# Projections in straight code with x turned a chunk ahead, and attention's first group loaded in the projection stage

## The reference

```
Q = x @ Wq ; K = x @ Wk ; V = x @ Wv          # Wq, Wk 256x512, Wv 256x256; 16 heads of 2*16 for Q, K
attn = softmax(Q1 K1^T * s) - lamb * softmax(Q2 K2^T * s)
x = layernorm(x + layernorm'(attn V @ Wo))
x = layernorm(x + moe(x))                     # 8 experts, top 2, 256 -> 1024 -> 256
```

## Time and profile before

| | us |
|---|---|
| median of 3 runs | 3537.51 |
| the profiled execution | 3536.64 |
| its span | 3534.9 |
| first projection matmul | 19.83 |
| last PE work of the projection stage starts | 185.64 |
| first instruction of the attention stage | 191.17 |
| first score matmul | 212.56 |
| first transposed scores of the main loop's lead | 266.01 |

### The profile page before, as it was taken

The page is one execution under the profiler, slowest core; times in us unless marked ns, Lnnn a source line. Parts: engine busy times, 40 slices in busy tenths (PEclk is TensorE's granted clock), DMA queues, the critical chain, the costliest instruction groups (busy, mean ns, idle before and its releaser), DMA issues. The chain is left out here.

```text
span 3534.9 us, 85163 instructions
## 1 busy us (share of the span) xinstructions
PE 3161.3 (89%) x29393; PEld 1464.0 (41%) x29394; DVE 2871.0 (81%) x3275; ACT 2510.3 (71%) x4642; POOL 415.4 (12%) x572
## 2 busy tenths in 40 slices
PE   7849999999999999999999999999993645999995
PEld 3413333333333333333333333333332534999994
DVE  2269999999999999999999999999995766343344
ACT  3308998998999899899989999989991101333331
POOL 0020000000000000000000000000002321555543
PEclk9969999999999999999999999999996766999997
DMA  4420101011010101101011010110107333222224
GB/s 116 119 54 14 26 8 30 8 26 30 8 29 8 27 13 25 27 11 26 9 29 26 11 27 8 29 27 8 29 8 249 143 122 120 37 37 37 36 37 113
DMA packets 100696, 154.36 MB, mean 44 GB/s; under 512 B 22488, under 2 KB 71432, under 8 KB 97484
## 3 DMA queue, kind: packets, MB, share of 16 engines
q1 hardware_dynamic: 84396, 130.44, 14.3%
q0 software_dynamic: 15904, 18.66, 3.2%
HBM read 92.81 MB, written 56.24 MB: 42 GB/s over the span
## 5 line engine op out<-in xcount | busy, mean ns | idle before, releaser
L544 DVE TENSOR_REDUCE half_max<-scores 128x2 f32<-128x1024 f32 x2096 | 2387.5, 1212 | 82.9 <-PE scores L447 79.2
L518 ACT ACTIVATE probs<-bank 128x512 f32<-128x512 f32 x4104 | 2226.9, 594 | 215.7 <-PE bank L466 147.5
L498 PE MATMUL bank<-probs,V 128*32 128x256 f32 x16384 | 1320.1, 394 | 70.3 <-ACT probs L518 39.2
L447 PE MATMUL scores<-K,Q 48*128 48x512 f16 x4192 | 832.8, 394 | 50.6 <-DVE half_max L544 24.6
L466 PE MATMUL bank<-Q,K 50*128 50x512 f16 x4104 | 798.3, 381 | 0.6 <-ACT probs L518 0.6
L447 PEld LDWEIGHTS scores<-K,Q 48*128 48x128 f16 x4192 | 201.3, 93 | 940.8 <-DVE half_max L544 737.3
L498 PEld LDWEIGHTS bank<-probs,V 128*32 128x32 f32 x16384 | 323.4, 108 | 630.8 <-issue 545.7
L466 PEld LDWEIGHTS bank<-Q,K 50*128 50x128 f16 x4104 | 375.9, 94 | 120.6 <-ACT probs L518 9.8
L1234 PE MATMUL pre<-xgT,w 128*128 128x128 f32 x2272 | 270.6, 278 | 4.2 <-ACT xgT L1264 4.2
L1234 PEld LDWEIGHTS pre<-xgT,w 128*128 128x128 f32 x2272 | 269.6, 195 | 8.8 <-issue 4.8
L417 POOL TENSOR_SCALAR max_parts<-row_max 128x16 f16<-128x16 f32 x65 | 16.5, 254 | 2160.8 <-DVE row_max L550 2160.8
(11 more groups left out here) (170 smaller groups left out, 1170.2 us busy)
## 6 DMA issues: line engine op xcount, KB each, us to landing
heads<-attended SPq DMA_DIRECT2D x5, 4096.0 KB, 13.0
attended<-att SPq DMA_DIRECT2D x64, 256.0 KB, 2.4
W<-in_L_ffn_w_dram SPq DMA_DIRECT2D x16, 1024.0 KB, 11.6
Q<-q_parts SPq DMA_DIRECT2D x96, 128.0 KB, 5.3
K<-k_parts SPq DMA_DIRECT2D x96, 128.0 KB, 5.6
q_parts<-parts SPq DMA_DIRECT2D x64, 128.0 KB, 2.4
k_parts<-parts SPq DMA_DIRECT2D x64, 128.0 KB, 2.4
join_x<-in_L_attn_x_dram SPq DMA_DIRECT2D x5, 1024.0 KB, 15.3
```

What stands on the lines that cost most here:

```text
L447: mm = nc.tensor.matmul(scores[:, b, h, :], Q[p][r, c, up, t * P:(t + 1) * P], K[p][r, up, kc * TC:(kc + 1) * TC], start=True, stop=True)
L498: mm = nc.tensor.matmul(banks[att_bank[s // KB]][32 * u:32 * u + 32, q], V[wp][:, wk, u // 2, :], probs[:, 4 * s % RING + u, q], start=(wk ...
L518: nc.scalar.activation(probs[:, i % RING, :], banks[tile_bank[i]][:], ACT.Exp, scale=SCALE).then_inc(exp_done, 1)
L544: nc.vector.tensor_reduce(half_max[lc % 2][:, :, up, t, kc], scores[:, b], AX.X, ALU.max).then_inc(max_done[b], 1)
```

## The change

The arrays `Q`, `K`, `V` are made outside of both stages, so that the projection stage can fill them. In the projection stage:

- the loops over chunks are Python loops on every engine, and the semaphores count from 0 and no longer from 1;
- `xT` has two buffers. The turning of chunk n + 1 and its copies stand between items 3 and 4 of chunk n;
- x of chunk 0 is loaded before Wv, DVE's balance waits for Wq and Wk alone, and PE turns chunk 0 and computes its values around the balance;
- POOL's memsets and presets of `K` and `V` stand behind the identity matrix;
- SP loads all of the first group's `Q0` and `K0` with 12 DMAs of 128 KB in the middle of chunk 4; the attention stage has no load and no wait for them.

```
     sp.dma_start(wraw[:, :, 0, :], Wq...).then_inc(wqk_loaded, 16)
     sp.dma_start(wraw[:, :, 1, :], Wk...).then_inc(wqk_loaded, 16)
     load_x(0)
+    sp.dma_start(wv[:], Wv...).then_inc(wv_loaded, 16)
+    for n in range(NC):
+        if n == 0:
+            sp.wait_ge(x_turned, 1)
+            load_x(1)
+        for i in range(ITEMS):
+            if i == TURN_AT and n + 2 < NC:          # TURN_AT = 4
+                sp.wait_ge(x_turned, n + 2)
+                load_x(n + 2)
+            if i == TURN_AT and n == CH:
+                load_first_group()
+            sp.wait_ge(lo_ready, n * ITEMS + i + 1)
...
+def load_first_group():
+    for s in range(4):
+        sp.wait_ge(parts_stored[s], 32 * CH * (ITEMS // 4))
+    sp.wait_ge(ones_set, 4)
+    for h, i in ROWS:                                # 6 of them: one DMA for Q[0], one for K[0]
...
 @block.gpsimd
+    pool.wait_ge(ident_ready, 1)
+    for i in range(2):
+        for h in range(2):
+            nc.gpsimd.memset(K[i][HALF * h + 32:HALF * h + 64], ONE).then_inc(ones_set, 1)
...
 @block.scalar
+    copy_xT(0)
+    copy_values(0)
+    for n in range(NC):
+        for i in range(ITEMS):
+            if i == TURN_AT and n + 1 < NC:
+                copy_xT(n + 1)
...
+        if n >= 1:
+            copy_values(n)
 @block.tensor
+    pe.wait_ge(ident_ready, 1)
+    turn_x(0)
+    pe.wait_ge(w_peaked, 2)
     for m in range(2):
         mm = nc.tensor.transpose(pj[2][0:1, ...], w_peak[:, m:m + 1], ident[:])
     mm.then_inc(peaks_turned, 1)
+    pe.wait_ge(wv_loaded, 16)
+    pe.wait_ge(xT_ready, KD)
+    times_wv(0, range(1))
     pe.wait_ge(lift_bits_ready, 1)
     pe.wait_ge(row_set, 1)
     nc.tensor.matmul(pj[3][:, 0:2], one_row[:], lift_bits[:]...)
+    times_wv(0, range(1, TPC))
     pe.wait_ge(wqk_ready, 4 * KD)
+    for n in range(NC):
+        pe.wait_ge(xT_ready, KD * (n + 1))
+        for i in range(ITEMS):
+            if i == TURN_AT and n + 1 < NC:
+                turn_x(n + 1)
+            if n * ITEMS + i >= 4:
+                pe.wait_ge(lo_ready, n * ITEMS + i - 3)
...
+        if n >= 1:
+            times_wv(n, range(TPC))
 @block.vector
-    dve.wait_ge(w_loaded, 48)
+    dve.wait_ge(wqk_loaded, 32)
...
 stage_attend
-    sp.wait_ge(ones_set, 4)
-    for h, i in ROWS: ... first_loaded, rest_loaded (30 DMAs)
-    pool: four memsets of K, the presets of V, pool.wait_ge(v_preset, 4)
-    pe.wait_ge(first_loaded, QKD)
-    pe.wait_ge(rest_loaded, QKD * 3 // 2)
```

More of the change, by code:

```diff
@@ L102, in stage_project @@
     ITEMS = 2 * MC
+    NC = NB * CH
+    TURN_AT = ITEMS // 2
     with ExitStack() as ctx:
@@ L108, in stage_project @@
         xs = sb("xs", [P, TPC, D], F32)
-        xT = sb("xT", [P, KD, TC], F32)
+        xT = [sb(f"xT{i}", [P, KD, TC], F32) for i in range(2)]
         parts = sb("parts", [P, 4, 2, TC], F16)
@@ L171, in _, with copy_xT @@
         @block.scalar
         def _(act):
[L173 to L189, removed]
+            def copy_xT(n):
+                act.wait_ge(x_turned, n + 1)
+                if n >= 2:
+                    act.wait_ge(proj_ready, ITEMS * (n - 1))
+                    act.wait_ge(v_ready, 2 * (n - 1))
+                for k in range(KD):
+                    nc.scalar.copy(xT[n % 2][:, k, :], pxT[k][:]).then_inc(xT_ready, 1)
@@ new lines, in copy_values @@
+            def copy_values(n):
+                b, c = n // CH, n % CH
+                for j in range(TPC):
+                    act.wait_ge(v_ready, 2 * n + j // 2 + 1)
+                    nc.scalar.copy(values[:, b * G:(b + 1) * G, c * TPC + j, :],
+                                   pv[j // 2][:, j % 2, :].rearrange("p (g f) -> p g f", g=G)
+                                   ).then_inc(values_ready, 1)
+            copy_xT(0)
[4 more added lines that the diff above has]
+                        copy_xT(n + 1)
+                    act.wait_ge(proj_ready, n * ITEMS + i + 1)
+                    done = n * (ITEMS // 4) + i // 4
+                    if done > 0:
+                        act.wait_ge(parts_stored[i % 4], 32 * done)
+                    nc.scalar.copy(parts[:, i % 4, 0, :], pj[i % 4][:]).then_inc(hi_ready, 1)
+                if n >= 1:
+                    copy_values(n)
@@ L191, in _ @@
         @block.tensor
         def _(pe):
[L193 to L201, removed]
@@ L209, in _, with times_wv @@
                 mm.then_inc(x_turned, 1)
-                pe.wait_ge(xT_ready, KD * (n + 1) + 1)
-                for i in range(ITEMS):
-                    pe.wait_ge(lo_ready, n * ITEMS + max(i - 3, 0) + 1)
+            def times_wv(n, tiles):
+                for j in tiles:
+                    if n >= 1 and j % 2 == 0:
+                        pe.wait_ge(values_ready, TPC * (n - 1) + j + 2)
                     for k in range(KD):
[L215 to L221, removed]
+                        mm = nc.tensor.matmul(pv[j // 2][:, j % 2, :], xT[n % 2][:, k, j * P:(j + 1) * P], wv[:, k, :],
                                               start=(k == 0), stop=(k == KD - 1), skip_group_check=True)
@@ L257, in _ @@
                             lift[:, m:m + 1], None, ALU.mult).then_inc(wqk_ready, 1)
-            with dve.Fori(0, NB * CH) as n:
+            for n in range(NC):
                 for i in range(ITEMS):
@@ L291, in stage_attend @@
         banks = [ps(f"bank{i}", [P, TC], F32) for i in range(4)]
[L292 to L295, removed]
+        names = ("row_max_ready", "high_ready", "max_parts_ready", "max_blocks_ready", "max_rows_written",
+                 "scoresT_ready", "exp_done", "pv_done", "att_copied", "v_copied")
+        (row_max_ready, high_ready, max_parts_ready, max_blocks_ready, max_rows_written,
+         scoresT_ready, exp_done, pv_done, att_copied, v_copied) = (sem(n) for n in names)
         scores_ready = [sem(f"scores_ready{i}") for i in range(2)]
```

111 lines of the change are left out of this document (57 added, 54 removed).

## The result

The changed kernel takes 3482.84 us in the median of 4 runs (3482.36 to 3485.91), the kernel before 3538.6 beside it (3534.34 to 3541.44): a ratio of 0.9845, 95% interval 0.9828 to 0.9862. The profiled execution takes 3482.52 with a span of 3480.8, 54.1 us shorter than the span before. Faster was forecast, to 3488, with 3480 to 3500 as range; 49.0 us of gain were forecast and 54.1 found in the spans. One execution of the changed kernel in a later set took 3982.77 us at a granted clock of 0.731; it is left out of every time given here.

A forecast was written before the change was run, and what follows sets the result against it. PE was taken to bound the projection stage, with 22 us at the stages' border where nothing that bounds the kernel is done. Savings of 18.7 + 9.0 + 21.3 = 49.0 from 3537.5 gave 3488.5, forecast as 3488, range 3480 to 3500.

The forecast's parts named there:

- signs of being wrong: PE waits in chunk 5 for ACT or DVE, scaling takes over 2.2 us, or the first reduction starts after 166.
- Chunks: Projection chunks 1 to 7: the wait of 2.60 goes, a chunk takes 18.4 for 20.93; 18.7 us saved.
- The rival that the wait only moves: Projections: PE waits for `xT` or a bank elsewhere, 18 us of gain lost, time 3506; 4 in 100.
- The start: Up to chunk 1: projections start at 18.7, warm, chunk 1 at 33.7 for 42.73; 9.0 us saved.
- DVE beside POOL's memsets: At the start: DVE's reduction and scaling beside 14.18 us of memsets cost 0 to 2.2 us, taken as 0.
- The loads: First group's 12 loads in chunk 4: ACT waits 2 us, PE not; cost 0, or 10 if they stretch.
- a rival that had PE wait 9 to 10: Chunk 5: loads delay item 4's stores to 26 instead of 14, PE waits; time 3498; 12 in 100.
- the 14 of the forecast: Item 4's stores of chunk 4 land 14 us after chunk 5's transposes end: 0.5 + 12 + 1.5.
- The border: Between the stages: memsets and loads go, DVE starts at 191.8 for 213.21; 21.4 us, taken as 21.3.
- the warm entry: Attention's main loop: PE stays warm through the score pairs ahead of it, saving 3.9 us, time 3484; 10 in 100.
- Slower by a falling clock: Projections: the clock falls under an unbroken float32 stream; 3634 if all eight chunks run at half clock; 2 in 100.
- The bounds: The whole sum: 3485 (9.9, 18.9, 21.8 saved) to 3494 (8.0, 15.2, 20.3), 2 more for the scaling.

The follow-up runs named there:

- one-`xT` kernel: The changed kernel with a single xT buffer: PE turns each chunk at its own start and waits for ACT's copies, in straight code; 3491.59 us.
- the pieces: The changed kernel with POOL's four memsets of K cut into 64 short ones at the same place beside DVE's chain; 3481.39 us.
- border undone: The changed kernel with POOL's memsets and presets and the first group's loads back at the start of the attention stage; 3492.56 us.
- both edits: The changed kernel with POOL's memsets behind DVE's scaling and the 12 loads spread, one behind every second item; medians 3477.52 and 3472.88 us.

## Why the prediction was right, and which of its terms were off

The number was right; of the mechanism, three of its own signs of being wrong came true. PE waited in chunk 5 for DVE, 2.63; the scaling took 2.29, more than 2.2, if barely; and the first reduction started at 169.15, after 166. The terms together were forecast at 49.0, and the places they speak of gave 44.1, 46.9 and 45.0 in the change's three profiles, against the same profile before. The spans gave 54.1, 59.7 and 45.8. What lies between, 10.0, 12.8 and 0.8 us, was in no term.

*Chunks.* A wait of 2.60 at each border goes, PE is what is late next: shown by the one-`xT` kernel and the profile after. A chunk takes 18.07 where I wrote 18.4. Its parts are 13.74 of projections (13.83 in the earlier trace rows), 3.45 of values, and 0.88 for the transposes in their middle (from 28.92 to 29.80), not 1.04 and a hop. Six chunks gave 2.0 more than forecast. The dips at the borders are gone, as forecast. The rival that the wait only moves did not come: PE waits once in the stage, in chunk 5, and not seven times.

*The start.* Forecast 18.7 for the first projection, measured 22.06; the failed term is "DVE beside POOL's memsets, 0 to 2.2, take 0". It cost 4.1 in the profile with the memsets moved away, outside the bounds. (ACT's table load went the other way: it now comes at the stage's start, so `xT` was ready at 10.8 and not at 12.8. That let the first values start earlier, which shortened nothing, since the exponents came later still.) I had bounded the scaling, by its size, and left out the chain of small steps, whose price has nothing to do with their size: each `tensor_scalar` ended when the memset did, at 12.4, 15.9 and 16.9. And the argument from the rate, 0.93 element per ns, was false: beside short memsets the scaling was held too (3.15 for 2.20). Nor were the two rates like measures: the copy moves its 2048 elements of a partition in one instruction, the scaling 256 in each of eight, and a `tensor_scalar` of two elements takes 0.16 by itself. A slow rate does not show that an instruction leaves POOL alone; the rule of the mode in which the two collide, which the prediction weighed and set aside, is what the pieces agree with.

The Trainium skill (SBUF — State Buffer, "Who interferes with whom") says that DVE and GpSimd share one pair of ports as an exclusive lock, held for a whole instruction, and that `tensor_scalar` can take it, `tensor_tensor` only against reads. The profile after agrees: 3.27 us for a step of 0.16 beside a memset of 3.50, 0.22 unchanged for the `tensor_tensor`. By that page the term was there to be had; I weighed another page's rule for the scaling alone.

*The loads.* Forecast at 0, with a rival that had PE wait 9 to 10 (12 in 100). Measured: item 4's store let ACT go at 118.08, 19.3 after the transposes of chunk 5 were done (98.76), between the 14 of the forecast and the 26 of the rival. PE waited 2.63, 1.21 and 2.06 in three profiles of the change, and in two of them ran at half clock afterwards: 16 records in 8.83, 1.80 more. So the rival's mechanism was real and its price 1.5 to 4.6. Two parts of the 14 were too small. SP was to start on the loads 0.5 behind the transposes and started 2.6 behind them (101.34), since it first had item 3's stores and the next x to issue; the forecast had only item 3's stores in front. And from there the 12 loads and the store behind them took 16.7, not 12 and 1.5. The 12 was read from loads without company. The stores of items 0 to 3 are not what stood in the way, for item 3's landed 2.4 after their issue, and x is little of it, by the kernel with one `xT`; what makes up the rest is open.

*The border.* 21.4 forecast, 21.3 taken, 21.8 in the first profiles and 21.3 by the kernel with the border undone. The term of the best size, since each of its parts had a row.

*The main loop.* I kept its entry as it was, and the warm entry as a rival. The clock did fall during the pairs ahead of the loop (0.50 from 175 to 225 us), as before. The 1.2 us of the third milestone fit the slow steps behind it: three where there were four and a half, 0.87 each. The 6.1 us at the turns were in no term. Without them the first profile would have given 48.0. That it lies near 49.0 is partly luck: the misses of 3.4 at the start and 4.6 in chunk 5 were met by 2.4 in the other chunks, 0.5 at the border, 1.2 at the loop's entry and 2.7 behind the loop, of which only the first two belong to the change for certain.

*Slower by a falling clock.* Refuted: in the kernel with both edits PE works from 16.54 to its last values without a wait, at full clock.

*The bounds.* The low end of the sum is misadded: 9.9, 18.9 and 21.8 make 50.6, and 3537.5 less that is 3487, not 3485. The range of 3480 to 3500 does not hang on it.

## What to carry to other kernels

Work moved to an idle engine is not free if it shares something with the engine on the path: look for short instructions with the price of a long one, and move the filler behind the chain, or cut it small. A row of loads put into a steady stream of stores costs by how late the store behind it lands; the same 12 loads, one behind every second item, cost nothing. And where a loop has turns at which the clock falls, compare stages by their milestones: single executions of one kernel differ by more than the edit is worth.

## What the runs showed of the hardware

- A `tensor_scalar` of DVE on one partition and two elements took 3.27 us beside a POOL memset of 3.50 and 0.24 to 0.27 beside memsets of 0.31, 0.16 alone; `tensor_reduce` (2.35) and `tensor_tensor` (0.22) beside the same memsets were as fast as ever.
- PE at float32 without a pause for 140 us kept the granted clock at 1.00; waits of 1.99 (memsets in pieces), 2.06, 2.63 and 2.65 in chunk 5 were followed by half clock, waits of 1.21, 1.67 and seven of 1.16 were not. In the kernel before, of the seven waits of 2.6 to 2.7 ahead of chunks 1 to 7 two were (as at 63.66 in the earlier trace rows) and five were not.
- The time that seven turns of one loop cost went from 37.2 to 47.5 us in three executions of the same program.
- What stays open: why PE's idle time at these turns adds up to 31 us in the kernel before and to 25 to 27 with PE's projections in straight code, why that did not shorten the turns, and what makes the 12 loads take longer beside the stores.
